# Attention over gathered keys and values: three of a quad's four gathers also wait for a share of ScalarE's weighing of the next quad

## The reference, cut to what matters

```python
q, k, v = (feats @ W.T + b for each of the three), split into 8 heads
sim  = einsum('hed,hed->eh', q[:, c, :], k[:, r, :]) * scale     # r = src, c = dst
p    = exp(sim - segment_max(sim, c)[c])
attn = p / segment_sum(p, c)[c]
agg  = segment_sum(attn * v[:, r, :], c)
out  = x + agg @ Wo.T + bo
```

## Time and profile before

| | us |
|---|---|
| median of three runs | 7130.53 |
| span of the profiled execution (first to last instruction) | 7184.9 |
| attention stage in it, from the profile's windows | about 3815 to 6980 |
| GpSimd busy in that stage | 1851.23 |
| VectorE busy in that stage | 2228.56 |
| ScalarE busy in that stage | 2079.80 |
| TensorE matmuls busy in that stage | 2158.61 |

### The profile page before, as it was taken

One profiled execution on the slowest core, in us unless ns is written; L12 is line 12 of the kernel. 1 busy time (PEld: TensorE's weight loads), 2 busy tenths in 40 slices (PEclk: granted clock), 3 DMA queues, 4 the chain that ended last, 5 costly groups with the idle time before them and its releaser, 6 DMA issues. The chain is left out here.

```text
span 7184.9 us, 117508 instructions
## 1 busy us (share of the span) xinstructions
PE 4609.9 (64%) x19717; PEld 3407.0 (47%) x19717; DVE 4538.0 (63%) x12295; ACT 3961.0 (55%) x14482; POOL 4666.6 (65%) x3716
## 2 busy tenths in 40 slices
PE   1456666666666666657885666676666766766767
PEld 1344444444444445544553444454444544544545
DVE  4665555555555666655546767777666767776766
ACT  0655555555555555533334666666666666666661
POOL 1488888888888888885554555666565655665630
PEclk6677777777777777778997887888877888888779
DMA  8777777777777777778754665666665666666646
GB/s 310 179 105 105 105 105 106 106 105 108 105 108 108 107 108 109 109 94 295 259 190 138 172 173 167 185 179 182 181 182 172 183 183 188 183 186 188 193 134 194
DMA packets 644181, 1130.07 MB, mean 157 GB/s; under 512 B 74529, under 2 KB 466795, under 8 KB 643445
## 3 DMA queue, kind: packets, MB, share of 16 engines
q0 software_dynamic: 367600, 678.97, 48.4%
q1 hardware_dynamic: 223985, 273.78, 11.8%
q10 hardware_dynamic: 51860, 169.74, 7.2%
HBM read 929.80 MB, written 451.51 MB: 192 GB/s over the span
## 5 line engine op out<-in xcount | busy, mean ns | idle before, releaser
L701 POOL DMA_INDIRECT sums<-mtw,posIw x1563 | 2490.8, 1594 | 599.4 <-issue 416.2
L1249 POOL DMA_INDIRECT kv<-kvt,sI x1760 | 1802.6, 1024 | 1247.1 <-issue 1107.1
L1610 ACT ACTIVATE room<-kv,pp 128x33 f32<-128x33 f32 x8800 | 1921.3, 308 | 47.8 <-issue 43.4
L1525 PE MATMUL ps<-room,Of 128*128 128x264 f32 x3520 | 1193.8, 484 | 619.6 <-DVE acc L1713 455.5
L734 PE MATMUL ps<-h,wf 128*128 x3320 | 1225.0, 524 | 307.1 <-DVE mtw L825 238.5
L718 PE MATMUL ps<-Mw,Oh 128*128 128x128 f32 x3320 | 671.9, 368 | 916.5 <-DVE Oh L852 908.7
L1525 PEld LDWEIGHTS ps<-room,Of 128*128 128x128 f32 x3520 | 760.4, 233 | 911.8 <-issue 585.3
L825 DVE SCALAR_TENSOR_TENSOR mtw<-mtw,cont,ps 128x256 f32 x1660 | 794.6, 479 | 621.2 <-SPq L690 448.1
L718 PEld LDWEIGHTS ps<-Mw,Oh 128*128 128x128 f32 x3320 | 631.5, 274 | 1033.8 <-DVE Oh L852 993.9
L734 PEld LDWEIGHTS ps<-h,wf 128*128 128x128 f32 x3320 | 818.5, 263 | 589.2 <-issue 450.0
L799 ACT COPY wf<-ps 128x512 f32<-128x512 f32 x415 | 242.8, 585 | 1237.8 <-PE ps L718 933.3
(11 more groups left out here) (223 smaller groups left out, 4741.1 us busy)
## 6 DMA issues: line engine op xcount, KB each, us to landing
qb<-qt SPq DMA_DIRECT2D x880, 192.0 KB
accd<-acc SPq DMA_DIRECT2D x880, 132.0 KB
ints<-srows ACTq DMA_DIRECT2D x205, 512.0 KB
OT<-drows SPq DMA_DIRECT2D x110, 512.0 KB
sums<-zero ACTq DMA_DIRECT2D x72, 704.0 KB
part<-sums SPq DMA_DIRECT2D x56, 896.0 KB
kv<-kvt,sI POOLq DMA_INDIRECT x1760
kvt<-kvo SPq DMA_DIRECT2D x98, 260.0 KB
```

What stands on the lines that cost most here:

```text
L701: e.indirect_dma_start(sums[t % NS], bass.IndirectOffsetOnAxis(ap=posI[:, t % NP:t % NP + 1], axis=0), mt[:, t % NM, :], None, compute_op= ...
L1249: e.indirect_dma_start(kv[:, s % NK, :], None, kvt, bass.IndirectOffsetOnAxis(ap=sI[:, s:s + 1], axis=0)).then_inc(kvs.sem(s), 16)
L1525: m = e.matmul(psum[6 + j % 2][:, 0:NH * 33], lhsT=Of[:, w % 2, k % W2, :], rhs=pv[:, k % NV, :], start=(k % 2 == 0), stop=(k % 2 == 1))
L1610: e.activation(pv[:, s % NV, h * 33:h * 33 + 33], kv[:, s % NK, D + h * 33:D + h * 33 + 33], ACT.Copy, scale=pp[:, w % 2, h, s % W2:s % W2 ...
```

## The change: what it does

For each quad g from 11 on, the second, third and fourth gather each get a wait of their own on `l_wact`, the count of ScalarE's activations. `before` is the count when quad g-11 is done. Gather i (1, 2, 3) waits for i quarters of ScalarE's activations of quad g-10 on top of it. The first gather of each quad is issued as before.

```diff
                         if g >= NK // 4:
                             wait_weighed(e, g - NK // 4)
                         for s in range(max(NE, 4 * g), 4 * g + 4):
+                            if g >= NK // 4 and s % 4:
+                                before = NH * weighed(1, g - NK // 4)
+                                e.wait_ge(S("l_wact"), before + s % 4 * NH * len(shares(g - NK // 4 + 1)[1]) // 4)
                             gather(e, s)
```

## The result

The changed kernel took 6945.9 us as the median of 4 runs (6937.8 to 6951.8), beside 7130.0 us for the kernel before (7118.9 to 7140.3). The ratio is 0.9737 (95% interval 0.9722 to 0.9752), which is 184 us less where I forecast 124. In a later group of runs, on the chip numbered 4 (the record does not number the first one), it was 0.9771 (0.9749 to 0.9793). And in groups of runs on three further chips the kernel before took 6356 to 6376 us, and the part of the change that I could try there brought nothing. That is the larger finding, and the experiments come to it.

The account below looks back on a forecast made before the run. Attention was taken to be bound by a loop of waits, with TensorE's results late while gathers stream. Gains of 177 us less 28 and 25 gave -124 us on the profiled span, 7007 us as median, range 6840 to 7165.

Parts of the forecast that it names:

- What bounds the stage: Attention: a loop of waits; TensorE's results come late while gathers stream; a stop lasts allowed gathers times 1.25 us plus 2.
- The waits themselves: GpSimd in attention: some 1287 new waits cost 0, with 6.4 us of each 28.5 us window to spare.
- Term 1: In front of `tops`: one gather (52) moves behind it, so 67 held windows stop 1.25 us less, 84 us in 104 windows.
- Term 2: In front of `lim`: two gathers (68, 74) move behind it, 36 stops 2.3 us shorter, 83 us in 104 windows.
- Price 1: Between `tops` and `lim`: gathers start 0.9 us earlier and catch the result of `spread` in 7 windows, costing 28 us.
- Price 2: Behind `exp`: three gathers start later where it waits for really late work, and the run before `tops` too, costing 25 us.
- Price 3: Product of a quad (L1667): its gathers come up to some 4 us later but are issued well ahead, costing 0.
- (b): In front of `tops`: ten gathers where there were eight make the run 1.1 us longer a window, 7251 us; chance 0.19.
- (a): Stops in attention come from something other than gathers, so nothing changes, 7130 us; chance 0.12.
- (c): Attention: with shorter stops VectorE runs on and fewer results meet traffic, a gain of 350 us, 6783 us; chance 0.09.

Follow-up runs that it names:

- the six inner ones: Kernel before plus only the waits for activations 22, 28, 34, 44, 48 and 62, which cross no place where ScalarE waits for TensorE: ratio 0.9988.
- the gather of mark 52: Kernel before with one new wait a window, the fourth gather of its quad waiting for activation 52, behind `tops`: ratio 0.9941, 42 us less.
- the six crossing waits: Changed kernel with only the waits for activations 52, 68, 74, 84, 88, 92, against the kernel before on quick chips: ratios 0.9997 and 0.9990.
- The four parts measured alone: Kernel before plus only some waits, by activation: 52, 0.9941; 68 and 74, 0.9884; 84, 88 and 92, 1.0001; 22, 28, 34, 44, 48 and 62, 0.9988.
- the tiny rows: Kernel before with gathers behind the first 44 bringing 104 bytes a row in place of 2080, on quick chips: ratios 1.0121, 1.0114 and 1.0089.

## Why the prediction was right, and where not

*What bounds the stage.* Right in the main for the kind of chip that was profiled: the loop of waits, with results of TensorE that come late while gathers run and, in front of `tops`, mostly come free some 2 us after the last. Shorter runs in front of `tops` and `lim` did shorten the stops. Two things I had wrong. I wrote it as a property of the kernel, and it is one of the kernel on some chips. And I took a result to be late whenever gathers stream, with a stop as long as the run; but whether it is late hangs on how far the run has come, 16% late at the first two gathers and 92% from the fifth on. A run that is moved changes how many results are caught and not only for how long.

*The waits themselves cost nothing.* Right as far as measured: the six inner ones give 9 us, within the noise. The six others were not priced apart from what they move.

*Term 1, `tops`, 89 us.* The mechanism was right in part, the size of it not. My 1.25 us was for each held window, 0.8 us over all. Alone, the gather of mark 52 shortens `exp` to `tops` by 1.3 us over all windows, with stops 2.1 us shorter and 20 more of them, but more than that comes back in front of `exp`, and 42 us are left. In the whole change this part falls by 2.4 us a window in the first profile and by 1.7 in the second, two to three times what I gave it: 49 windows of 103 now have no remote stop in front of `tops`, where it was 37 of 104, and the stops that are left last 5.1 us, not 6.8. I had counted on shorter stops and not on fewer; of the 182 us that the remote idle time fell (to 276, where I forecast about 380), about half is either.

*Term 2, `lim`, 88 us of the same 177.* Alone the number was right, 83 us, and in part by luck: the remote idle time in front of `lim` fell by 163 us, through fewer stops as well as shorter ones, and the rest was given back at other places. In the whole change it does not show at that place. The stops are shorter by 1.9 us (I gave 2.3), but there are 52 of them, not 36, and the idle time is 286 us where I forecast about 190.

*Price 1, gathers that start earlier behind `tops`, 7 windows.* This was mis-sized: 16 more windows are caught at `lim`, at my 4 us each 64 us and not 28.

*Price 2, the three gathers behind `exp`, 25 us.* It did not come: 1.0001 (0.9990 to 1.0012), so between 7 us gained and 9 us lost.

*Price 3, the product's gathers, 0.* Right, 0.3 us of idle time as before. On the quick chips there is less cover: with the six crossing waits the product stood idle for gathers for 90.4 us in 77 steps there.

The four parts measured alone add up to 133 us (42 + 83 - 1 + 9), near my 124. The whole gives 184 us on the first chip and 164 on chip 4. Whether the 30 to 50 us on top come from the parts acting together is not shown: the intervals of the four parts leave some 33 us either way on their sum (root of the sum of squares, with the chips taken as alike), the whole was measured on other chips, and the kernel that was to split it ran on chips without stops, twice. So that the inner waits matter once the others are there is not excluded either. The nearness of the forecast to the result is partly luck: `tops` brought more than I gave it, `lim` nothing at its place, and the 25 us of price 2 did not come.

*The rivals.* (b), a longer run in front of `tops`, did not come: ten gathers have their marks there, and `exp` to `tops` fell. (a), that the stops have another cause, is refuted as far as shorter runs give shorter stops, and upheld in one respect: streaming gathers alone do not hold anything, since on a quick chip they stream at the same step and nothing is held. What the chips with stops have besides is open. (c), a larger gain with fewer results that meet traffic, is the way in which the result differs from the forecast, at half of the 350 us that I gave it.

The Trainium skill ("TensorE: Matmul & The Clock Gate", The cost: per-tile semaphore tail) prices a matmul's increment at some 26 ns. On the quick chip the trace agrees that it is tens of nanoseconds, with a median of 14 ns from a matmul's recorded end to its semaphore. On the chips with stops it does not: a result was 10.6 us behind its record, and the median from the fifth gather of a run on is 4.7 us. The prediction says that no row shows so short a tail in a run of gathers; the trace has them there too, at the first two gathers above all.

## What to carry to other kernels

Where an engine waits for a result that is long there by the records, lay the timeline of the engine that streams DMAs beside it: if most stops end about the same time after the last DMA of a run, count how many DMAs are allowed to start before the place of the wait, and move some behind it. Move those that cross a place with stops; waits that cross no place gave nothing clear of noise, and neither did those that cross `exp`, where there were hardly any stops. Then count the stops again, at every place: the ones that are left can be more. And measure such a change on more than one chip before it is called a gain: here it is 2.3 to 2.6% on one kind and 0 to 0.1%, for the crossing waits, on the other.

## What the runs showed of the hardware that was not expected

- The same program takes 7130 to 7172 us on some chips and 6356 to 6376 us on others; within a group the runs of that kernel lie within 0.7% of each other. The difference lies in attention: from the first `exp` to the last it is 3102 us in the profile of the kernel before and 2306 us in that of the six crossing waits on a quick chip, 796 of the 828 us between the two spans. Gathers, VectorE's and ScalarE's instructions take the same time on both (an activation 308 and 307 ns, a gather 1.03 and 0.99 us).
- TensorE's granted clock over the stage is 0.81 on the kind with stops and 0.94 on the quick kind, and 1.00 in the run without gathers. In a pause after a stop it is at 0.50, the level of 1.2 GHz, behind a stretch in which TensorE had nearly stood still (busy for 0.27 us from 5468 to 5474). I take it for a consequence of the stops: while the result of the earlier trace rows began to be held, from 5456 to 5468, the clock was at 1.00, the level of 2.4 GHz, and in the first 3700 us of the program it is 0.75 on either kind of chip. No run here changes the clock alone.
- On a quick chip, leaving all gathers out gains only 2.1%, and the stage is then bound by VectorE, busy for 2158 of 2175 us:

```profile
3815.00:5990.00 2175.00, 1830.90 (x10506) 1301.98 (x10507) 2157.95 (x3589) 2046.17 (x9497) 69.86 (x109) 1.00 0.15 45
```

- Moving a twentieth or half of the bytes with the same number of gathers made the program 0.9 to 1.2% slower on those chips, not faster. In the profile of the tiny rows `lim` waits for its matmul for 326 us in all:

```profile
L1642 ACT COPY lim<-ps 128x2 f32<-128x2 f32 x110 | 17.3, 157 | 326.4 <-PE ps L1556 326.4
```

  There is no profile of the kernel before on a quick chip to set beside it. The six crossing waits, which take the same time as that kernel there, have 3.9 us from `tops` to `lim`, the tiny rows 6.7. Why it is slower stays open.
